# Head 0 alone in the prologue of a transformer layer on eight Trainium2 cores

## The reference, cut to what matters

```
# x: (4, 2048, 2048) float32; 16 heads of 128; FFN 2048 -> 5632 -> 2048
def attn(x):                       # q_w, k_w, v_w, o_w: 2048 x 2048; gate_w: 128 x 128
    q, k, v = proj(q_w), proj(k_w), proj(v_w)
    scores = causal(einsum('bhqd,bhkd->bhqk', q, k) / sqrt(128))
    av = einsum('bhqk,bhkd->bhqd', softmax(scores), v)
    gate = sigmoid(einsum('bhqd,ed->bhqe', q, gate_w) + gate_b)
    return einsum('bsd,ed->bse', merge(av * gate), o_w)

def ffn(x):                        # ternary weights with scales
    g = (x @ gate_w.T) * gate_s
    u = (x @ up_w.T) * up_s
    return ((silu(g) * u) @ down_w.T) * down_s

x = x + layernorm(attn(layernorm(x)))
x = x + layernorm(ffn(layernorm(x)))
```

## Time and profile before

| | |
|---|---|
| median of 3 runs | 1744.88 us (1744.62 to 1745.45) |
| the profiled execution | 1746.27 us |
| its span on the slowest core (core 0) | 1744.7 us |
| spans of the eight cores | 1739.5 to 1744.7 us |
| TensorE matmuls busy, core 0 | 1672.8 us, 96% of the span |
| VectorE, ScalarE busy, core 0 | 561.1 and 369.7 us |
| mean granted TensorE clock | 0.989 to 0.995 of full |

### The profile page before, as it was taken

How to read it: one execution, slowest core, us unless ns; L and a number is a source line. 1 busy time by engine, 2 the same in 40 slices (tenths; PEclk the granted TensorE clock), 3 DMA queues, 4 the chain that set the end, 5 groups by cost and what they waited for, 6 DMA issues and landing times.

```text
span 1744.7 us, 29210 instructions; the slowest of 8 cores (1739.5 to 1744.7 us)
## 1 busy us (share of the span) xinstructions
PE 1672.8 (96%) x11796; PEld 1109.6 (64%) x11796; DVE 561.1 (32%) x1250; ACT 369.7 (21%) x615; POOL 127.2 (7%) x244
## 2 busy tenths in 40 slices
PE   4889999999999899999999999999999999999996
PEld 2556777677675444666666666666666688888742
DVE  4345555555566466211111111111111011111144
ACT  4334334443434222211111111111111000000022
POOL 0000000000000000000000000000002111111000
PEclk9999999999999999999999999999999999999998
DMA  9343345334303333544434434334435545444466
GB/s 239 80 85 62 62 78 91 52 61 85 61 15 85 120 145 128 121 73 73 68 59 68 73 69 76 59 64 73 73 71 97 100 70 70 72 69 74 79 218 194
DMA packets 44348, 153.17 MB, mean 88 GB/s; under 512 B 5040, under 2 KB 6320, under 8 KB 39600
## 3 DMA queue, kind: packets, MB, share of 16 engines
q0 software_dynamic: 34560, 102.78, 35.1%
q1 hardware_dynamic: 9648, 48.45, 8.4%
HBM read 235.09 MB, written 18.87 MB: 146 GB/s over the span
## 4 chain that ended last, share of the span: by engine, by line
PE 92%; DVE 3%; DMA 2%; issue 1%; ACT 1%; ACTq 0%; DVEq 0%; SPq 0%; POOLq 0%
PE psum L356 91%; PE psum L361 2%; DMA xin<-x_l 1%; DMA a_wb<-wq_d 1%; DVE a_Bb L531 1%; DVE psum L594 1%; DMA cf<-cf_d 0%; ACT a_h1b L404 0%; DVE a_V L494 0%; DVE st L381 0%; ACT L367 0%; DVE a_xb L873 0%; DVE a_yb L1114 0%; ACT a_h2b L885 0%; ACT a_absq L514 0%
## 5 line engine op out<-in xcount | busy, mean ns | idle before, releaser
L356 PE MATMUL psum<-a_h2T,a_fw 128*128 128x384 bf16 x4128 | 671.3, 326 | 0.0
L356 PEld LDWEIGHTS psum<-a_h2T,a_fw 128*128 128x128 bf16 x4128 | 403.9, 98 | 266.8
L356 PE MATMUL psum<-a_wd,a_hdn 128*128 128x256 bf16 (+1 forms) x2772 | 345.2, 288 | 0.7 <-DVE a_hdn L951 0.7
L356 PEld LDWEIGHTS psum<-a_wd,a_hdn 128*128 128x128 bf16 x2772 | 271.1, 98 | 74.5 <-issue 1.0
L356 PE MATMUL psum<-a_h1T,a_wb 128*128 128x384 bf16 x1536 | 295.8, 329 | 5.7 <-DMA a_wb<-wq_d 4.2
L951 DVE SCALAR_TENSOR_TENSOR a_hdn<-psum,cf,a_sg 128x384 bf16<-128x384 f32 x132 | 81.5, 618 | 595.8 <-PE psum L356 591.6
L356 PEld LDWEIGHTS psum<-a_h1T,a_wb 128*128 128x128 bf16 x1536 | 147.9, 99 | 94.2 <-issue 10.3
L942 ACT ACTIVATE a_sg<-psum,cf 128x384 bf16<-128x384 f32 x132 | 76.5, 581 | 592.9 <-PE psum L356 592.9
L598 ACT ACTIVATE a_P<-psum 128x512 bf16<-128x512 f32 x192 | 109.4, 570 | 252.7 <-DVE psum L594 224.7
L356 PE MATMUL psum<-a_wb,a_h1T 128*128 128x256 bf16 x1152 | 153.0, 277 | 1.8 <-DMA a_wb<-wv_d 1.8
L594 DVE TENSOR_TENSOR psum<-psum,a_Bb 128x384 f32<-128x384 f32 (+3 forms) x240 | 114.9, 479 | 69.1 <-PE psum L356 68.6
(11 more groups left out here) (76 smaller groups left out, 827.4 us busy)
## 6 DMA issues: line engine op xcount, KB each, us to landing
a_fw<-wg_d POOLq DMA_DIRECT2D x43, 512.0 KB, 5.1
a_fw<-wu_d POOLq DMA_DIRECT2D x43, 512.0 KB, 6.2
a_wd<-wd_d POOLq DMA_DIRECT2D x66, 256.0 KB, 4.4
xin<-x_l SPq DMA_DIRECT2D x9, 1024.0 KB, 16.3
a_xb<-x_l SPq DMA_DIRECT2D x9, 1024.0 KB, 4.9
y_d<-a_xb SPq DMA_DIRECT2D x9, 1024.0 KB, 3.9
a_yb<-y_d SPq DMA_DIRECT2D x9, 1024.0 KB, 6.9
a_wb<-wv_d POOLq DMA_DIRECT2D x16, 512.0 KB, 8.0
```

What stands on the lines that cost most here:

```text
L356: return self.q.do("T", lambda e: e.matmul(out, lhsT, rhs, start=start, stop=stop, skip_group_check=True), waits, tok)
```

## The change

- `prologue` now makes the K and Q of head 0 only. `fillers` gives head 0 the K and Q of head 1, as every other head has them. A running count (`debt`) gives each tile its share of the columns of head 0, as far as the chunk's last tile has come.
- In a round of the prologue TensorE now gets `back(t)`, the V of tile t-1, and then the chunks. The V of the last tile stands behind all chunks.
- The weights are asked for at other tiles: both halves of V with tile 0, K0 with tile 1, Q0 with tile 2 (role B: 6), the gate with tile 4 (B: 7), K1 with tile 7 (B: 14), Q1 and the next V with tile 8 (B: 15). The gate weight is converted by the DMA, in GpSimd's queue.
- The root is split from the reciprocal: VectorE's reciprocal and minus mean of tile t+2 stand behind its evacuation of V.
- Tile 0 is scaled in halves, one by ScalarE and one by VectorE.
- V alternates between banks 4 and 5, chunks between 6 and 7, and the three `gen_sum` of head 0 use three banks.
- ScalarE's list has no instruction ahead of the branch. Its table of Sqrt is asked for by a Sqrt of a constant 1.0 right behind the branch, the table of Exp by an Exp of 1.0 three rounds before the end of the prologue, and that of Sqrt again by a Sqrt at the start of `out_proj`.

```diff
     def fillers(self, s):
...
-        if 1 < nh < H:
+        if nh < H:
             out += [self.gen_k(nh, c) for c in range(len(r.KGROUPS))]
...
     def load_x(self, t):
         w = [self.x_cast[t - 4]] if t >= 4 else []
+        if t == 4:
+            w.append(self.x0_half)
...
-        tn = self.norm(mv, [ta, self.c_tok])
-        self.x_mv[t] = self.minus_mean(mv, tn)
+        self.x_sq[t] = self.spread(mv, [ta, self.c_tok])
+
+    def x_norm(self, t):
+
+        mv = self.k["mv"][t % 4]
+        self.x_mv[t] = self.minus_mean(mv, self.root(mv, self.x_sq[t]))
...
-            h1[:, :], x[:, :], ACT.Identity, scale=mv[:, 2:3],
+            h1[:, 0:n], x[:, 0:n], ACT.Identity, scale=mv[:, 2:3],
             bias=mv[:, 4:5]), w)
+        if t == 0:
+            self.x0_half = self.q.do("V", lambda e: e.tensor_scalar(
+                h1[:, n:], x[:, n:], mv[:, 2:3], mv[:, 4:5], ALU.mult,
+                ALU.add), w)
...
     def prologue(self):
...
+        for key, t in ((("v", 0, 0), 0), (("v", 0, 1), 0), (("k", 0), 1),
+                       (("q", 0), r.Q0 and 6 or 2), ("gate", r.Q0 and 7 or 4),
+                       (("k", 1), r.NK - 2), (("q", 1), r.NK - 1),
+                       (("v", 1, 0), r.NK - 1), (("v", 1, 1), r.NK - 1)):
+            after.setdefault(t, []).append(key)
...
+        def chain():
+            gens = [(a + n - 1, 0, c) for c, (a, n) in enumerate(r.KGROUPS)]
+            gens += [(r.Q0 + a + n - 1, 1, c)
+                     for c, (a, n) in enumerate(r.GROUPS)]
+            for last, kind, c in sorted(gens):
+                g = (self.gen_q if kind else self.gen_k)(0, c)
+                while self.seen_tile < last:
+                    yield 0
+                yield from g
...
+        per = 128 * KC * (r.NK + r.NQ) // r.NK
...
+            self.seen_tile = t - 1
+            if t < r.NK:
+                for x in self.gen_v(0, t - 1, 1):
+                    pass
+            if t + 2 < r.NK:
+                self.x_norm(t + 2)
+            if t + 2 == r.NK - 1:
+                q.do("S", lambda e: e.activation(
+                    k["mv"][2][:, 7:8], k["mv"][2][:, 6:7], ACT.Exp))
+            debt += per
+            while debt > 0 or t == r.NK:
+                x = next(work, None)
+                if x is None or x == 0:
+                    break
+                debt -= x
...
     def out_proj(self):
...
+        mv = self.k["mv"][3]
+        q.do("S", lambda e: e.activation(mv[:, 7:8], mv[:, 6:7], ACT.Sqrt))
...
     def build(self):
...
-        q.do("S", lambda e: e.activation(k["mv"][3][:, 7:8], k["eps"],
-                                         ACT.Sqrt), [self.c_tok])
         self.common = {e: len(q.ops[e]) for e in q.ENGS}
+        ones = [q.do("V", (lambda i=i: lambda e: e.memset(
+            k["mv"][i][:, 6:7], 1.0))()) for i in (2, 3)]
+        q.do("S", lambda e: e.activation(
+            k["mv"][3][:, 7:8], k["mv"][3][:, 6:7], ACT.Sqrt), ones)
```

More of the change, by code:

```diff
@@ L364, in norm, with spread, root @@
     def norm(self, mv, waits):
-        q = self.q
-        t = q.do("S", lambda e: e.activation(
+        return self.root(mv, self.spread(mv, waits))
+    def spread(self, mv, waits):
+        return self.q.do("S", lambda e: e.activation(
             mv[:, 3:4], mv[:, 1:2], ACT.Sqrt, bias=self.k["eps"]), waits)
-        return q.do("V", lambda e: e.reciprocal(mv[:, 2:3], mv[:, 3:4]), [t])
+    def root(self, mv, t):
+        return self.q.do("V", lambda e: e.reciprocal(
+            mv[:, 2:3], mv[:, 3:4]), [t])
     def minus_mean(self, mv, t):
@@ L754, in prologue, with weights @@
     def prologue(self):
-        r = self.r
-        chunks = []
-        for h in range(2):
-            for c, (a, n) in enumerate(r.KGROUPS):
-                chunks.append((a + n - 1, h, "k", c))
-            for c, (a, n) in enumerate(r.GROUPS):
-                chunks.append((r.Q0 + a + n - 1, h, "q", c))
-        chunks.sort(key=lambda x: (x[1], x[0]))
-        q, k = self.q, self.k
-        tg = q.dma("Y", k["gwf"][:, :], self.d["gw"])
-        bound = False
-        def run(c):
-            _, h, kind, i = c
-            for x in (self.gen_k if kind == "k" else self.gen_q)(h, i):
-                pass
-        self.cast([self.x_in[0]])
+        r, q, k = self.r, self.q, self.k
+        self.ring, self.ring_at = [6, 7], 0
+        ng = len(r.GROUPS)
+        after = {}
+        for key, t in ((("v", 0, 0), 0), (("v", 0, 1), 0), (("k", 0), 1),
[3 more added lines that the diff above has]
+            after.setdefault(t, []).append(key)
+        def weights(t):
+            for key in after.get(t, []):
+                if key == "gate":
+                    self.gw_dma = q.dma("GD", k["gwb"][:, :], self.d["gw"],
+                                        [self.x_in[t]])
+                else:
+                    self.cast([self.x_in[t]])
+        def chain():
[7 more added lines that the diff above has]
+                yield from g
+        self.seen_tile = -1
+        work = chain()
+        per = 128 * KC * (r.NK + r.NQ) // r.NK
+        debt = 0
+        weights(0)
         self.x_stats(0)
+        self.x_norm(0)
         self.scale(0)
         self.x_stats(1)
+        self.x_norm(1)
         for t in range(r.NK + 1):
@@ L795, in prologue @@
                 continue
-            n = 0
-            for c in list(chunks):
-                last, h, kind, i = c
-                if last > t - 1 or self.no[kind, h] >= len(self.cast_tok):
-                    continue
-                if n < 2 or t == r.NK and h == 0:
-                    n += 1
-                    chunks.remove(c)
-                    run(c)
-            if not bound and not any(c[1] == 0 for c in chunks):
-                bound = True
-                for g in [self.gen_max(0)] + [self.gen_abs(0, c) for c in
-                                              range(len(r.GROUPS))]:
-                    for x in g:
-                        pass
-            for x in self.gen_v(0, t - 1, 1):
-                pass
-        for c in chunks:
-            run(c)
-        for c in range(len(r.GROUPS)):
-            for x in self.gen_sum(0, c):
+            self.seen_tile = t - 1
[13 more added lines that the diff above has]
+                debt -= x
+        for g in [self.gen_max(0)] + [self.gen_abs(0, c) for c in range(ng)]:
+            for x in g:
+                pass
+        for x in self.gen_v(0, r.NK - 1, 1):
+            pass
+        for c in range(ng):
+            for x in self.gen_sum(0, c, (6, 7, 4 + r.NK % 2)[c]):
                 pass
-        self.ring, self.ring_at = [6, 7], 0
     def load_xb(self, t, waits):
```

32 lines of the change are left out of this document (14 added, 18 removed).

## The result

Five runs of the changed kernel have a median of **1733.6 us**, against 1745.02 for five of the kernel before on the same chip: a ratio of 0.993, 95% interval 0.9917 to 0.9943. It is faster, and inside the range, but the gain is 11.4 us where I forecast 18. (Some runs of most kernels here had one die at a lower granted clock, 0.82 to 0.98, and took 1762 to 2034 us; ratios and means leave them out, but for two of before at 1762 and 1763 us in the ratios of the first four experiments.)

A forecast was written before the change was run, and what follows sets the result against it. TensorE was taken as the bound after the prologue. Role B's 7.9 + 8.4 + 1.3 = 17.6 us took core 1 from 1744.5 to 1726.9; plus 1.57, less 1.39, 1727 us (forecast band 1722 to 1731; range 1721 to 1735).

The forecast's parts named there:

- The work that moves, the tiles: Prologue: head 1's projections move into head 0, 19.9 us on role B, 15.6 on role A; tile step stays 4.29 us.
- Head 0: Role B's head 0: 8.9 us are lost in it; filled like head 1, it gives 8.4 us back.
- The output projection: Both roles, first tile's transposes: loading the table earlier cuts the 5.41 us wait to 4.1, gaining 1.3 us.
- The start of role B: Start of the prologue: ScalarE ready at 14.11 us, first transpose at 17.9, first V projection at 25, gaining 7.9 us.
- Core 1 as role B: Whole span: role B forecast from core 1, 17.6 us gained, from 1744.5 to 1726.9 us.
- Role A: Whole span, core 0: 2.4 + 6.9 + 8.6 + 1.3 = 19.2 us gained, from 1744.7 to 1725.5 us.
- The median: Whole kernel: the median of runs would be 1.39 us below the profiled execution.
- Rival 1: Role B's start: ScalarE's branch stays late, V starts 4 to 7 us later, 1731 to 1734 us; chance 0.13.
- The later the fuller the DMA engines were: Role B's branch: engines got through at 8.55, 14.11 and 21.55 us, later with fuller DMA engines; argued for Rival 1.
- rival 2: Prologue start: weights asked for sooner take DMA time from x tiles 2 to 5, 1730 to 1733 us; chance 0.07.
- Rivals 3 and 4: Head 0 gives nothing back, 1731 to 1735 us, chance 0.05; prologue tiles at the lower clock, 1767 us, chance 0.02.

The follow-up runs named there:

- the first four experiments: The first four follow-up runs on the changed kernel, timed beside 15 runs of the kernel before; no single time is given for them together.
- e4_fill_only: Kernel before plus moved head 1 projections, new weight order, banks and gate conversion; root, tile 0 scaling and table loads not changed; 1739.11 us, 0.9955.
- e12_undo_two: Changed kernel with two parts undone: roots waited for at once, no early Exp table in the prologue; one run, 1735.33 us.
- e2_act_common: Changed kernel with ScalarE's first root, and so its table load, put back ahead of the branch; 1735.39 us, 0.9923 of before.
- e5_v_common: Changed kernel with both weight loads of the first V group moved ahead of the branch; 1733.39 us, 0.9927 of before.
- e10_swap: Changed kernel with the roles' code in the other order, role B's first behind the branch, role A's second; 1733.89 us, 0.9937 of before.
- e9_order: e8 with VectorE's copy of tile t put behind the statistics of tile t+2 and ahead of its reciprocal; 1727.67 us, 0.9900 of before.
- e6: Changed kernel with tile t+1 scaled on ScalarE ahead of the copy of tile t's transposed half; one run, 1731.73 us.
- e7: e6 with the first V group's evacuation moved from VectorE to ScalarE; 1733.78 us, 0.9934 of before.
- e8: e7 with the V weights also asked for ahead of the branch; 1730.63 us, 0.9918 of before.
- e1_x_late: Changed kernel with SyncE's loads of x tiles 1 to 3 moved behind the branch; two runs average 1737.6 us.
- e1b_x23_late: Changed kernel with only the loads of x tiles 2 and 3 moved behind the branch; median 1738.53 us, 0.9948 of before.

## Why the prediction was right, and where it was not

- **The work that moves, the tiles:** right. 19.9 us forecast from the fifth tile to the bound on role B, 20.2 measured; tile step 4.29, forecast 4.29; nothing for the root, 0.35 measured.
- **Head 0:** right. 8.4 us forecast to come back. Less the 19.9 that moved in, 36.9 becoming 48.1 is 8.7. I had laid 3.67 of it to the wait behind the table; by e4_fill_only and e12_undo_two the table is worth 0.9 to 1.3 (more where the clock falls behind the wait) and the filling the rest.
- **The output projection:** right, 1.3 forecast, 5.41 to 4.13 measured. The 2.66 us of the Trainium skill ("ScalarE: Activation LUTs", What ACT_TABLE_LOAD costs) was not borne out here.
- **The start of role B: the step that failed.** 7.9 us forecast, 3.2 measured as the mean of role B (on core 1 itself 4.4 at the first V and 5.5 at the fifth tile). I took ScalarE's readiness right, with some luck, since it waits for VectorE there, and held all else where the earlier trace rows had it. VectorE's statistics were ready by about 11 us there, since VectorE had come through at 8.55. At 12.0 they are on the path, and a stall of 1.8 to 3.2 us in VectorE's list with them: first transposes at 19.8 us on the mean of role B where I had 17.9. From there to V I had 6.8 us; it was 8.5, since V waits for its weights: GpSimd asked for the second half at 17.0 us on core 1 (14.8 before), and it took 11.3 us to land. I had that landing wrong too: the 8.9 us of the earlier trace rows are the middle of the two halves, 7.6 and 10.2, so even by the rows of before the data stood at 25.0 and not 23.7. Why VectorE and GpSimd crossed later than before (12.0 for 9.6 us, and 15.8 for 14.2) stays open, and a part may be scatter: by e2_act_common it is not ScalarE, and by e5_v_common, with VectorE at 12.4, not the V weights. Nor has any run with this tile step met the forecast. My 17.9 and 25 us put the fifth tile of core 1 at 45.3 - 7.9 = 37.4; e10_swap, with a first tile at 12.5, has it at 38.5 (37.9 at the earliest), since the transfers stand under it. Only core 7 of e9_order came to 37.4.
- **Core 1 as role B: the second half of the miss.** Its 45.3 us at the fifth tile were the latest of four (the others 41.1 to 43.5), and its span of 1744.5 stands over 1740.3 to 1741.9 for its sisters. Taking 17.6 us off it gave 1726.9 and was nearly met (1727.7), in part by luck: it gained 5.5 us up to the fifth tile, 9.2 in head 0 and 2.1 behind it. The others had less to lose. Core 7 went from 1741.5 to 1729.9. Core 0 was the same kind of high draw (1744.7; the role's mean 1741.3, and 17.5 us gained where core 0 gained 21.8). The time is a maximum over four role-B starts that scatter anew in each run.
- **Role A:** 19.2 us forecast, 17.5 measured as its mean. Its V projection gained nothing (26.6 us as before, forecast 2.4). From there to the first gate 7.3 us came off beyond the 15.6 that moved (forecast 6.9), and in the two heads 8.5 (forecast 8.6). Role A does not end last, so its miss cost nothing.
- **The median** is 2.1 us above the profiled run; I had it 1.4 below, as it was for before. That is the same scatter.
- **Rivals.** Rival 1 was right that the start would disappoint, and right on the fetch (e10_swap), but wrong on the engine: ScalarE is early, VectorE and GpSimd are late, and ScalarE is not the cause (e2_act_common). "The later the fuller the DMA engines were" was a misreading: on core 1 of before their share is 0.90 to 1.03 from 2 to 21.6 us, at all three crossings. Of rival 2 the general part holds, that the transfers bound the first tiles. Rivals 3 and 4 did not occur; the tiles of 4.29 us ran at a granted 1.00.

## What to carry to other kernels

Where several cores run one role, forecast from the mean and the spread of the cores, not from the slowest of one profile: the slowest is a draw, and the next run draws again. Follow a gain at the start to the landmark where the transfers catch up before you book it. When a wait is filled by moving work, ask what covered the other waits: the early V weights were worth nothing alone and the reordered scale 1.5 us up to the bound, and with the next two steps they made the best version.

## What the runs showed of the hardware that I had not expected

- Where a role's code lies decides when it starts: 4.7 against 12.0 us for the same program (e10_swap, after), and 2 to 3 us at the end the other way.
- VectorE stood 1.8 to 3.2 us with the label "issue" between two instructions 0.27 us apart elsewhere (16.45 and 18.81 on core 1, 15.99 and 19.33 on core 7), on all role-B cores of the changed kernel; 1.6 to 3.4 us on those of e5, e6 and e12, and not at all in e7, e8 and e9, in which role A's code, which lies ahead, has nine instructions fewer on VectorE. In e10_swap it is role A, now the second body, that stands 2.9 to 3.8 us, two instructions earlier. In e1_x_late and e1b_x23_late, with VectorE's list unchanged and fewer x loads in flight, VectorE stands only 0.5 to 0.7 us at this place. A fetch in the middle of straight code could do this; no run tried it by itself.
- A transfer that is asked for sooner need not land sooner. On core 1 the second half of V's weights took 11.3 us in the changed kernel, asked for at 17.0, 16.7 in e10_swap, asked for at 8.2, and 19.1 in e1_x_late, asked for at 12.1, where it landed 2.9 us later than in the changed kernel.
- Short drops of the granted clock make part of the scatter: core 1 of e10_swap had one where core 1 of the changed kernel had none, and its gate and up projections took 537.5 us instead of 535.8. Its window (TensorE busy, matmuls, then granted clock, DMA share, GB/s):

```profile
920.00:940.00 20.00, 17.90 (x103) 0.91 0.81 171
```
